# Perceiver block on one core: the experts' weight split moved into the cross-attention, five value copies moved to ScalarE, new instruction orders, a shorter rsqrt

## The chip, the cores and the metric
The kernel runs on 1 core of a Trainium2 chip. The metric is the device time of one execution in microseconds. Three runs of the kernel before took 1942.69, 1944.77 and 1945.35 us (median 1944.77).

## The reference
Three residual steps on x of 32 x 64 tokens of width 256:

```
x = x + cross_attention(layernorm(x), ctx, mask)   # ctx 32 x 1601 x 256, 16 heads of 16, masked softmax over 1601 keys
x = x + gated_causal_attention(layernorm(x))       # attn * tanh(gelu(drift * g_w1 + g_b1) @ g_w2 + g_b2); drift = gelu(layernorm(x @ dp_w1)) @ dp_w2
x = x + moe(layernorm(x))                          # 8 experts, top 2 of them, silu(a) * g @ w2[e], hidden 704
```

Weights and inputs are 32-bit floats. The experts' weights w1 (8 x 1408 x 256) and w2 (8 x 256 x 704) are wanted in two 16-bit parts, high and low, so that products of parts replace products of 32-bit floats.

## The kernel before, in words
The program has a front part (layer norm, queries), the cross-attention, the self-attention with the gate and the router's product, the routing, and the experts. Within a part every engine runs an order that is written out by hand as a string of steps; semaphores tie the engines together. TensorE, ScalarE, VectorE, GpSimd and SyncE (the queue of transfers) each take their steps strictly in order.

The cross-attention runs 32 periods, one per batch entry b, with a lead-in. Period b does the attention (S, E, L, W) of entry b, the projections and maxima (K, V, M) of entry b + 1, and the preparation of the context of entry b + 2. The steps, by engine:

- TensorE (`PE_ORDER`): K0..K7 project a piece of the keys (L696), V0..V6 two tiles of values (L708), M0..M15 a pair of score blocks for the row maxima (L723), S0..S12 a tile of transposed scores (L743, L747), W0..W12 the product of weights and values (L764 to L769), T turns the maxima (L775). K, V, M and T write into three banks of `ring`; M takes banks 0 and 1, K and V one that `K_BANK` and `V_BANK` name. A step waits until the bank's last holder has been read.
- ScalarE (`ACT_ORDER`): KH keeps the high part of a key piece (L628), E makes two exponentials of a score tile, `pT` in 32 bits (L639) and `ph` in 16 (L641), CH the high part of a context chunk (L599).
- GpSimd (`POOL_ORDER`): L makes the low part `pl = pT - ph` (L405), CL the low part of the context (L399), ADD a residual.
- VectorE (`DVE_ORDER`): KL the low part of keys (L498), VH and VL the high and the low part of values (L483, L492), X the maxima with the mask added (L535), SH and SPR the shift of the scores (L545, L551), N the normalization of the entry before, MP the mask's conversion (L560).
- SyncE: in every period the context load, the stacking of queries, 12 transfers that stack the first half of the keys, the mask, the block queries, 12 transfers for the second half, and the shift.

E(n) waits for S(n) and W(n-3); S(n) for E(n-2); W(n) for L(n). M(n) waits for X(n-1). The next period's S0 waits for the shift, and with it for SPR.

In the self-attention the steps are those of `SELF_PE`, `SELF_ACT`, `SELF_POOL`, `SELF_DVE` and `SELF_SP` over 16 tiles of 128 tokens. WL (L899 to L903), HI (L1141), LW (L1054) and WS (L932) split the experts' weights there: 24 pieces of 128 x 1408, each loaded, its high part made on ScalarE, its low part on VectorE, both stored to device memory, with two buffers. MX are the scores for the maxima, RM reads them, T and MC turn them, SH is their transfer, S, E, W and O the attention, A, WO and R its output, SU and NU the next layer norm, TU, RT and RC the router's product. The experts' part (from 1670 us) waits for all stores.

`newton_rsqrt` (L202) makes 1/sqrt on VectorE in chained steps, each waiting for the one before; it is used once ahead of the cross-attention and eight times in the self-attention (N, HN and NU).

Of the kernel before, what the change touches and what calls it, by code (L numbers as in the profile page):

```python
# [159 lines left out]
def program(nc, a, out):  # L160
    with ExitStack() as ctx:
# [59 lines left out]
        with ExitStack() as c1:  # L221
# [85 lines left out]
            with nc.Block() as block:  # L307
                @block.sync
                def _(sp):
# [47 lines left out]
                    def period(b, i, j, do_a, do_b):  # L357
                        if has_later(b):
                            load_context(b + 2)
                        if do_b:  # L360
                            stack_queries(b + 1, 1 - j)
# [1385 lines left out]
```

## Time and profile before

| | us |
|---|---|
| median of three runs | 1944.77 |
| profiled execution | 1940.98 |
| its span, first to last instruction | 1939.2 |
| turn of the maxima, first and last | 115.2 and 1377.0 |
| self-attention, first product to the end of the part | 1427 to 1638 |
| mean granted TensorE clock | 0.941 |

The span is that of one execution under the profiler; the other numbers of the document's rows are times within it, counted from its first instruction. A row of the timeline has the start, the length, the engine, the line, the operation, what it writes and reads, and how many like it are merged; in brackets stand idle time before it and what ended it. TensorE's products are pipelined, so that the distance of the starts, not the length of a row, is what one unit costs.

### The profile page before, as it was taken

What the parts mean: (1) busy time and instruction counts of PE and PEld (TensorE: products, weight loads), DVE (VectorE), ACT (ScalarE), POOL (GpSimd) and SP (SyncE); (2) the same over time, 40 slices, a digit from 0 to 9 for tenths busy, and PEclk for the clock granted to TensorE, in tenths of its full rate; (3) what the DMA queues carried; (4) which work ended last, traced back from release to release, by engine and by line L of the source; (5) the groups of instructions that cost most, each with busy time, mean ns of one, the idle gap of its engine ahead of it and who ended that gap; (6) DMA issues with size and microseconds to landing.
All of it is one profiled execution on the core that took longest, in us unless ns stands there. A gap on an engine that the chain in (4) does not pass through costs nothing. (4 is left out here: it accounts for less than half of the span.)

```text
span 1939.2 us, 59104 instructions
## 1 busy us (share of the span) xinstructions
PE 1749.3 (90%) x24652; PEld 1155.3 (60%) x24673; DVE 1384.8 (71%) x3589; ACT 1298.0 (67%) x1595; POOL 1293.0 (67%) x669
## 2 busy tenths in 40 slices
PE   3789999999999999999999999999867886599996
PEld 1346666666666666666666666666533565488885
DVE  5568888888888888788888888888467576644442
ACT  2258788887888888888878888788745543133332
POOL 1248888988888888888888888888733200244432
PEclk9779999999999999999999999999778786699998
DMA  4444445444455454544445544444156675588884
GB/s 152 167 107 116 125 135 141 126 113 129 117 154 132 109 130 114 154 130 116 123 119 153 138 112 119 123 136 107 28 170 215 200 264 191 194 250 267 248 248 126
DMA packets 169867, 290.83 MB, mean 150 GB/s; under 512 B 56450, under 2 KB 136706, under 8 KB 169442
## 3 DMA queue, kind: packets, MB, share of 16 engines
q1 hardware_dynamic: 162114, 276.83, 49.0%
q0 software_dynamic: 7488, 10.23, 2.6%
q8 instruction: 196, 3.21, 0.7%
q14 instruction: 69, 0.57, 0.1%
HBM read 169.80 MB, written 33.16 MB: 105 GB/s over the span
## 5 line engine op out<-in xcount | busy, mean ns | idle before, releaser
L405 POOL TENSOR_TENSOR pl<-pT,ph 128x1024 f16<-128x1024 f32 x416 | 882.0, 2133 | 182.4 <-ACT ph L641 182.3
L535 DVE CUSTOM_DVE_ANT_0 junk<-ring,mbias 128x804 bf16<-128x804 f32 x512 | 507.3, 991 | 170.4 <-issue 159.8
L639 ACT ACTIVATE pT<-score,lift 128x1024 f32<-128x1024 f32 (+1 forms) x416 | 464.5, 1117 | 75.0 <-PE o_acc L769 38.0
L641 ACT ACTIVATE ph<-score,lift 128x1024 f16<-128x1024 f32 (+1 forms) x416 | 464.3, 1116 | 0.0
L708 PE MATMUL ring<-wvp,cp 128*128 128x256 f16 (+1 forms) x2496 | 311.2, 276 | 4.4 <-DVE kl L498 0.5
L696 PE MATMUL ring<-cp,wkp 128*128 128x402 f16 x1536 | 307.6, 337 | 5.2 <-DVE kst L464 1.8
L708 PEld LDWEIGHTS ring<-wvp,cp 128*128 128x128 f16 (+1 forms) x2496 | 236.4, 100 | 82.3 <-issue 50.0
L399 POOL TENSOR_TENSOR cp<-cx,cp 128x804 f16<-128x804 f32 x128 | 252.4, 1992 | 49.3 <-ACT cp L599 49.3
L723 PE MATMUL ring<-kh,qm 32*128 32x402 f16 x1024 | 265.2, 338 | 19.6 <-DVE mx L535 10.2
L628 ACT ACTIVATE kh<-ring,bks 128x402 f16<-128x402 f32 x256 | 155.2, 606 | 174.7 <-PE ring L696 174.7
L769 PE MATMUL o_acc<-v,pl 128*128 128x33 f16 (+1 forms) x3328 | 242.6, 179 | 0.1
L764 PE MATMUL o_acc<-v,ph 128*128 128x66 f16 x2912 | 221.5, 192 | 6.4 <-POOL pl L405 6.4
L764 PEld LDWEIGHTS o_acc<-v,ph 128*128 128x128 f16 x2912 | 182.3, 97 | 57.5 <-issue 41.5
L769 PEld LDWEIGHTS o_acc<-v,pl 128*128 128x128 f16 (+1 forms) x3328 | 213.8, 96 | 0.7
L696 PEld LDWEIGHTS ring<-cp,wkp 128*128 128x128 f16 x1536 | 131.2, 98 | 129.6 <-DVE kl L498 21.5
L747 PEld LDWEIGHTS score<-qst,kst 64*128 64x128 f16 x6656 | 157.6, 97 | 50.1 <-issue 2.7
L483 DVE CAST v<-ring 128x512 f16<-128x512 f32 (+1 forms) x224 | 144.9, 652 | 54.2 <-PE ring L708 51.1
L743 PE MATMUL score<-delta,mbias 64*128 64x512 bf16 (+1 forms) x832 | 164.6, 392 | 11.8 <-ACT ph L641 4.7
L498 DVE SCALAR_TENSOR_TENSOR kl<-ring,bks,kh 128x402 f16<-128x402 f32 x256 | 160.2, 634 | 18.2 <-ACT kh L628 13.7
L747 PE MATMUL score<-qst,kst 64*128 64x64 f16 x6656 | 168.4, 191 | 0.0
L1369 POOL DMA_INDIRECT acc_d<-ys,to_row x39 | 64.2, 1645 | 141.4 <-DVE ys L1540 72.5
L1636 PE MATMUL score<-xp,w1p 128*128 128x256 f16 (+1 forms) x1584 | 150.9, 254 | 3.4 <-DMA w1p<-wsp 3.0
(232 smaller groups left out, 2055.1 us busy)
## 6 DMA issues: line engine op xcount, KB each, us to landing
cx<-in_ctxT SPq DMA_DIRECT2D x32, 1601.0 KB
w1p<-wsp SPq DMA_DIRECT2D x24, 1408.0 KB, 8.2
kst<-kh SPq DMA_DIRECT2D x256, 100.5 KB, 2.9
msk<-in_mask SPq DMA_DIRECT2D x64, 400.2 KB, 5.5
kst<-kh SPq DMA_DIRECT2D x256, 99.6 KB, 2.5
wsp<-w_parts SPq DMA_DIRECT2D x24, 704.0 KB, 4.3
w2p<-wsp SPq DMA_DIRECT2D x24, 640.0 KB
kst<-kl SPq DMA_DIRECT2D x128, 100.5 KB, 2.7
```

The source lines that it names most:

```text
L399: pool.tensor_tensor(cp[:, j, 1, :, chunk(n)], cx[:, :, chunk(n)], cp[:, j, 0, :, chunk(n)], ALU.subtract).then_inc(cl_ready, 1)
L405: pool.tensor_tensor(pl[:, u].rearrange("p h q -> p (h q)"), pT[:, u], ph[:, u].rearrange("p h q -> p (h q)"), ALU.subtract).then_inc(pl_r ...
L535: dve.tensor_tensor_reduce(junk[:, n % 2], ring[:, 0:2, 0:KW], mbias[:, j, 2 * KW * half:2 * KW * half + 2 * KW].rearrange("p (c k) -> p c ...
L639: act.activation(pT[0:n, u].rearrange("k (h a q) -> k a h q", a=2, q=S), scored, ACT.Exp, bias=lift[0:n, 0:1], scale=SSCALE)
L641: act.activation(ph[0:n, u].rearrange("k h (a q) -> k a h q", a=2), scored, ACT.Exp, bias=lift[0:n, 0:1], scale=SSCALE).then_inc(exp_done, 1)
L696: mm = pe.matmul(ring[:, BANK["K", k], 0:KW], wkp[:, z, cc, P * t:P * t + P], cp[:, j, y, cc, chunk(c)], start=(cc == 0 and z == y), stop= ...
L708: mm = pe.matmul(ring[0:n, BANK["V", u], D * half:D * half + D], cp[:, j, z, cc, P * kt:P * kt + n], wvp[:, y, cc, :], start=(cc == 0 and ...
L723: mm = pe.matmul(ring[:, c, 0:KW], qm[rows, j, t], kh[rows, t, chunk(2 * half + c)], start=True, stop=True)
L743: pe.matmul(score[0:n, 2 * slot + side, :], mbias[part, j, rows], delta[part, :], start=True, stop=False, skip_group_check=True)
L747: mm = pe.matmul(score[0:n, 2 * slot + side, S * p:S * p + S], kst[part, j, p, rows], qst[part, j, p, :], start=False, stop=True, skip_gro ...
L764: pe.matmul(o_acc[:, at:at + 2 * PW], high, vv.rearrange("k z w -> k (z w)"), start=(kt == 0 and p == 0), stop=last, skip_group_check=True)
L769: mm = pe.matmul(o_acc[:, at:at + PW], low, vv[:, 0, :], start=False, stop=last, skip_group_check=True)
```

## The change
The experts' weights are loaded, split and stored during the cross-attention, one of the 24 pieces in each of the periods 0 to 23, with one buffer that lies where the front part's query and value weights lay. Of the seven value copies VH of a period, ScalarE takes the numbers 0, 1, 3, 4 and 6 (6 is a single tile, the others are two), VectorE keeps 2 and 5. SyncE's order in a period becomes a string as well, with the block queries behind the shift. All other orders are new, and so are the banks. `newton_rsqrt` folds a multiplication into a fused step: 13 steps, 12 of them waited for, instead of 15. The first layer norm of the self-attention scales its 16 tiles in three runs (0 to 4, 4 to 12, 12 to 16) instead of two.

```diff
-NEWTON = 15
+NEWTON = 13
-PE_ORDER = steps("K0 S0 K1 S1 K2 V0 K3 S2 K4 M0 S3 W0 M1 S4 W1 M2 V1 M3 W2 W3 S5 M4 K5 M5 S6 S7 M6 V2 W4 M7 W5 S8 M8 K6 "
-                 "M9 W6 S9 M10 K7 M11 S10 W7 M12 W8 S11 M13 V3 M14 S12 W9 W10 M15 V4 W11 T V5 V6 W12")
-ACT_ORDER = steps("KH0 E0 KH1 KH2 E1 KH3 E2 KH4 E3 E4 CH0 E5 KH5 CH1 E6 E7 E8 KH6 CH2 E9 KH7 E10 CH3 E11 E12")
+PE_ORDER = steps("K0 V0 K1 S0 K2 M0 S1 S2 M1 K3 M2 S3 W0 M3 K4 W1 M4 S4 V1 V2 W2 K5 M5 S5 S6 M6 K6 M7 W3 W4 M8 K7 M9 S7 "
+                 "S8 M10 W5 V3 W6 V4 S9 S10 W7 M11 V5 M12 S11 W8 M13 S12 W9 M14 W10 M15 V6 W11 T W12")
+ACT_ORDER = steps("KH0 VH0 KH1 E0 KH2 E1 KH3 E2 KH4 E3 VH1 E4 KH5 CH0 E5 KH6 HI E6 KH7 E7 E8 VH3 VH4 E9 E10 E11 E12 CH1 "
+                  "VH6 CH2 CH3")
 POOL_ORDER = steps("L0 ADD L1 L2 L3 L4 L5 CL0 L6 L7 L8 L9 L10 L11 L12 CL1 CL2 CL3")
-DVE_ORDER = steps("KL0 N KL1 KL2 VH0 VL0 KL3 X0 KL4 X1 X2 VH1 X3 VL1 X4 X5 KL5 X6 VH2 X7 VL2 X8 X9 KL6 X10 X11 KL7 X12 "
-                  "X13 VH3 X14 VL3 X15 SH VH4 SPR VL4 VH5 VH6 VL5 VL6 MP")
-K_BANK, V_BANK, T_BANK = (2, 1, 2, 1, 2, 2, 2, 2), (0, 2, 2, 2, 2, 0, 1), 1
+DVE_ORDER = steps("N VL0 KL0 KL1 X0 KL2 X1 X2 KL3 X3 KL4 X4 VL1 VH2 VL2 X5 KL5 X6 X7 KL6 X8 X9 KL7 X10 LW VL3 VL4 X11 "
+                  "X12 VH5 X13 MP X14 VL5 X15 SH VL6 SPR")
+SP_ORDER = steps("WL CTX STKA MASK STKB QST SHIFT QM WS")
+K_BANK, V_BANK, T_BANK = (1, 0, 2, 2, 2, 2, 2, 2), (2, 2, 0, 2, 0, 2, 2), 0
...
-SELF_SP = steps("CA0 CB0 RO0 WL0 WL1 SK0 WS0 WL2 WL3 WS1 SQ0 SK1 WS2 WL4 WL5 WS3 SQ1 SH0 SH1 SH2 WS4 WL6 WL7 WS5 SK2 "
...
+SELF_PE = steps("X0 X1 V0 K0 K1 Q0 Q1 V1 V2 V3 X2 X3 V4 K2 K3 X4 Q2 Q3 MX0 V5 V6 V7 T0 V8 V9 MX1 X5 X6 K4 MX2 K5 T1 T2 "
+                "MX3 S0 V10 S1 V11 V12 V13 MX4 T3 Q4 Q5 MX5 T4 S2 X7 T5 MX6 W0 T6 K6 S3 W1 K7 W2 S4 W3 A0 A1 A2 WO0 WO1 "
...
+                "WO14 A15 TU5 WO15 TU6 RT5 RT6 TU7 TU8 RT7 RT8 TU9 TU10 TU11 RT9 RT10 TU12 TU13 RT11 RT12 TU14 TU15 "
+                "RT13 RT14 RT15")
+SELF_SP = steps("CA0 RO0 CB0 SK0 SQ0 SK1 SQ1 SH0 SH1 SK2 SH2 SH3 SQ2 SH4 SH5 SH6 SK3 AS0 SQ3 XS0 SH7 SH8 SH9 SH10 SH11 "
+                "SH12 AS1 SH13 SH14 XS1 SH15 AS2 XS2 AS3 XS3")
...
+            dve.tensor_scalar(ve, ve, -0.5, None, ALU.mult).then_inc(s_newton, 1)
+            chain[0] = chain[0] + 1
             step(dve.tensor_scalar(y.bitcast(I32), t.bitcast(I32), -1, 0x5F3759DF, ALU.mult, ALU.add))
             for _ in range(3):
                 step(dve.tensor_tensor(t, y, y, ALU.mult))
                 step(dve.tensor_tensor(t, t, ve, ALU.mult))
-                step(dve.tensor_scalar(t, t, -0.5, 1.5, ALU.mult, ALU.add))
-                step(dve.tensor_tensor(y, y, t, ALU.mult))
+                step(dve.scalar_tensor_tensor(y, t, 1.5, y, ALU.add, ALU.mult))
...
+            w_whole = nc.alloc_sbuf_tensor_at("w_whole", [P, WP], F32, offset=spent)
+            w_parts = nc.alloc_sbuf_tensor_at("w_parts", [P, 2, WP], F16, offset=spent + 4 * WP)
...
+                    def load_whole(q):
+                        e, k = q // PIECES, q % PIECES
+                        if q == 0:
+                            sp.wait_ge(q_done, DC * NCH)
+                            sp.wait_ge(bv_added, 1)
+                        after(sp, w_low, q)
+                        if k < DC:
+                            sp.dma_start(w_whole[:], a["w1T"][e, P * k:P * k + P]).then_inc(w_in, 16)
...
+                            elif kind == "WS" and has_piece(b):
+                                sp.wait_ge(w_low, b + 1)
+                                sp.dma_start(wsp[b // PIECES, b % PIECES], w_parts[:]).then_inc(w_out, 16)
...
+                            elif kind == "LW" and has_piece(b):
+                                dve.wait_ge(w_high, b + 1)
+                                dve.scalar_tensor_tensor(w_parts[:, 1], w_whole[:], WSCALE, w_parts[:, 0], ALU.mult, ALU.subtract).then_inc(w_low, 1)
...
+                    def keep_vh(b, j, u):
+                        n = KROWS[2 * u]
+                        tiles = min(2, KT - 2 * u)
+                        act.wait_ge(v_done, b * VU + (u + 1))
+                        after(act, pv_done, (b - 1) * KT)
+                        act.activation(v[0:n, j, 2 * u:2 * u + tiles].rearrange("k t p z w -> k (t p) z w")[:, :, 0, 0:2 * DH],
+                                       ring[0:n, BANK["V", u], 0:tiles * D].rearrange("p (h w) -> p h w", w=2 * DH), ACT.Copy).then_inc(vh_there, 1)
...
+                            elif kind == "HI" and has_piece(b):
+                                act.wait_ge(w_in, 16 * (b + 1 + (b + 1) // PIECES))
+                                after(act, w_out, 16 * b)
+                                act.activation(w_parts[:, 0], w_whole[:], ACT.Copy, scale=WSCALE).then_inc(w_high, 1)
```

## Rows read from the trace of the kernel before

**Rows 1.** Busy time by stage: cross-attention, self-attention to W0, self-attention from W0; columns named.
```profile
core 0: us, PE busy (x) PEld busy (x) DVE busy (x) ACT busy (x) POOL busy (x), PEclk, DMA share, GB/s
116.00:1378.00 1262.00, 1240.07 (x19055) 784.19 (x19054) 1028.25 (x2656) 1047.52 (x1174) 1096.81 (x538) 1.00 0.47 126
...
1427.00:1504.00 77.00, 63.75 (x525) 33.08 (x532) 55.39 (x135) 39.21 (x58) 24.00 (x15) 0.88 0.68 220
1504.00:1638.00 134.00, 111.19 (x1968) 86.37 (x1968) 81.99 (x226) 66.17 (x97) 14.02 (x11) 0.78 0.70 229
```

**Rows 2.** The line of the turn of the maxima: ns min/median/max, first and last start.
```profile
L775 PE MATMUL ring<-fold,top_m x64: 219/243/317, 115.2 to 1377.0; 128*32 128x64 f32 x64
```

**Rows 3.** Timeline of TensorE in a period (start us, length us, what).
```profile
524.65 0.20 PE L764 MATMUL o_acc<-v,ph 65*128 65x66 f16 x1
...
525.12 1.18 PE L696 MATMUL ring<-cp,wkp 128*128 128x402 f16 x6
...
526.23 0.39 PE L743 MATMUL score<-delta,mbias 64*128 64x512 bf16 x2
...
526.79 1.19 PE L696 MATMUL ring<-cp,wkp 128*128 128x402 f16 x6
...
537.45 1.49 PE L708 MATMUL ring<-wvp,cp 128*128 128x256 f16 x12
...
538.87 0.51 PE L723 MATMUL ring<-kh,qm 32*128 32x402 f16 x2
...
542.63 0.51 PE L723 MATMUL ring<-kh,qm 32*128 32x402 f16 x2
...
543.07 0.39 PE L743 MATMUL score<-delta,mbias 64*128 64x512 bf16 x2
...
543.53 0.38 PE L743 MATMUL score<-delta,mbias 64*128 64x512 bf16 x2
...
544.24 0.51 PE L723 MATMUL ring<-kh,qm 32*128 32x402 f16 x2
...
544.88 1.47 PE L708 MATMUL ring<-wvp,cp 128*128 128x256 f16 x12
...
546.18 0.19 PE L764 MATMUL o_acc<-v,ph 128*128 128x66 f16 x1
...
546.74 0.51 PE L723 MATMUL ring<-kh,qm 32*128 32x402 f16 x2
```

**Rows 4.** Timeline of ScalarE in the same period: KH0, E0, KH1, E12.
```profile
526.40 0.60 ACT L628 ACTIVATE kh<-ring,bks 128x402 f16<-128x402 f32 x1 [4.43 <-PE ring L696]
...
526.90 1.11 ACT L639 ACTIVATE pT<-score,lift 128x1024 f32<-128x1024 f32 x1
...
528.91 0.60 ACT L628 ACTIVATE kh<-ring,bks 128x402 f16<-128x402 f32 x1
...
560.34 1.11 ACT L639 ACTIVATE pT<-score,lift 65x1024 f32<-65x1024 f32 x1 [0.31 <-PE o_acc L769]
```

**Rows 5.** Timeline of VectorE in the same period: VH1, X5, KL5.
```profile
538.97 0.69 DVE L483 CAST v<-ring 128x512 f16<-128x512 f32 x1 [0.41 <-PE ring L708]
...
543.18 0.99 DVE L535 CUSTOM_DVE_ANT_0 junk<-ring,mbias 128x804 bf16<-128x804 f32 x1 [0.61 <-issue]
...
544.10 0.63 DVE L498 SCALAR_TENSOR_TENSOR kl<-ring,bks,kh 128x402 f16<-128x402 f32 x1
```

**Rows 6.** Timeline of GpSimd in the same period: L12.
```profile
562.53 2.13 POOL L405 TENSOR_TENSOR pl<-pT,ph 128x1024 f16<-128x1024 f32 x1 [0.29 <-ACT ph L641]
```

**Rows 7.** All HI and LW, by the tile they write: ns min/median/max.
```profile
L1141 ACT ACTIVATE w_parts<-w_whole x24: 1359/1368/1378, 1442.3 to 1633.9; 128x1408 f16<-128x1408 f32 x24
...
L1054 DVE SCALAR_TENSOR_TENSOR w_parts<-w_whole,w_parts x24: 1603/1626/3637, 1443.7 to 1635.3; 128x1408 f16<-128x1408 f32 x24
```

**Rows 8.** All CL by line; then one CL and the MP beside it.
```profile
L399 POOL TENSOR_TENSOR cp<-cx,cp x128: 1702/1715/2877, 18.7 to 1342.6; 128x804 f16<-128x804 f32 x128
...
525.80 2.87 POOL L399 TENSOR_TENSOR cp<-cx,cp 128x804 f16<-128x804 f32 x1
...
526.12 0.98 DVE L560 TENSOR_SCALAR mbias<-msk 128x1601 bf16<-128x1601 int32 x1
```

More of the change, by code:

```diff
@@ L119 @@
 HT = TILES // 2
-SELF_PE = steps("X0 X1 V0 Q0 K0 K1 V1 X2 X3 V2 V3 V4 V5 V6 Q1 K2 K3 V7 Q2 Q3 X4 MX0 MX1 V8 V9 T0 MX2 T1 X5 X6 V10 T2 "
[6 rows of a table removed]
-SELF_ACT = steps("XN0 XN1 XN2 XN3 XC0 XC1 QH0 XN4 KH0 XN5 XN6 XN7 KH1 XC2 XN8 XC3 XN9 HI0 XN10 XN11 HI1 QH1 KH2 KH3 HI2 "
[6 rows of a table removed]
-SELF_POOL = steps("BO0 BO1 BO2 HG0 HW0 PR0 HM0 BO3 VG0 VG1 VG2 VG3 HG1 HW1 PR1 HM1 VG4 VG5 VG6 VG7")
-SELF_DVE = steps("ST0 ST1 ST2 ST3 N0 ST4 ST5 ST6 ST7 ST8 ST9 ST10 ST11 ST12 ST13 ST14 ST15 N1 QL0 VV0 KL0 HS0 KL1 VV1 "
[8 rows of a table removed]
-SELF_SP = steps("CA0 CB0 RO0 WL0 WL1 SK0 WS0 WL2 WL3 WS1 SQ0 SK1 WS2 WL4 WL5 WS3 SQ1 SH0 SH1 SH2 WS4 WL6 WL7 WS5 SK2 "
[3 rows of a table removed]
+SELF_PE = steps("X0 X1 V0 K0 K1 Q0 Q1 V1 V2 V3 X2 X3 V4 K2 K3 X4 Q2 Q3 MX0 V5 V6 V7 T0 V8 V9 MX1 X5 X6 K4 MX2 K5 T1 T2 "
[6 rows of a table added]
+SELF_ACT = steps("XN0 XN1 XN2 XN3 XC0 XN4 XN5 XC1 XN6 XN7 KH0 KH1 QH0 QH1 XC2 XN8 XC3 XN9 XN10 XN11 KH2 KH3 XC4 XN12 "
[5 rows of a table added]
+SELF_POOL = steps("BO0 BO1 BO2 BO3 HG0 HW0 PR0 HM0 VG0 VG1 VG2 VG3 HG1 HW1 PR1 HM1 VG4 VG5 VG6 VG7")
+SELF_DVE = steps("ST0 ST1 ST2 ST3 ST4 ST5 ST6 ST7 N0 ST8 ST9 ST10 ST11 N1 ST12 ST13 ST14 ST15 N2 VV0 KL0 HS0 KL1 QL0 "
[7 rows of a table added]
+SELF_SP = steps("CA0 RO0 CB0 SK0 SQ0 SK1 SQ1 SH0 SH1 SK2 SH2 SH3 SQ2 SH4 SH5 SH6 SK3 AS0 SQ3 XS0 SH7 SH8 SH9 SH10 SH11 "
+                "SH12 AS1 SH13 SH14 XS1 SH15 AS2 XS2 AS3 XS3")
 SELF_USES = [use for use in SELF_PE if use[0] in ("X", "Q", "K", "V", "T", "A", "TU")]
@@ L182, in program @@
         ln_ve, ln_y, ln_t = (sb(f"ln_{w}", [P, TILES]) for w in ("ve", "y", "t"))
+        spent = -(-nc.sbuf_base // 32) * 32
+        xn = sb("xn", [P, 2, D])
         xn_d = nc.dram_tensor("xn_d", (TOK, D), F32).ap()
@@ L252, in program @@
             hold_v = sb1("hold_v", [P, 2])
-            junk = sb1("junk", [P, 2, 2, KW], BF16)
+            junk = sb1("junk", [P, 2, KW], BF16)
             mx = sb1("mx", [P, PAIRS, 3])
@@ L285, in program @@
             x2_ready = sem("x2_ready")
+            w_in, w_high, w_low = sem("w_whole_in"), sem("w_high_parts"), sem("w_low_parts")
             CONSTS = [(ident[:], a["ident"]), (sel_q[:], a["sel_q"]),
@@ L302, in has_later, with has_piece @@
                 return not (isinstance(b, int) and b + 2 >= B)
+            def has_piece(b):
+                return 0 <= b < E * PIECES
             def chunk(n):
@@ L357, in period @@
                     def period(b, i, j, do_a, do_b):
[L358 to L361, printed above, removed]
-                            stack_keys(b + 1, 1 - j, 0)
-                        if has_later(b):
-                            load_mask(b + 2)
-                            load_block_queries(b + 2, j)
-                        if do_b:
-                            stack_keys(b + 1, 1 - j, 1)
-                            shift_queries(b + 1, 1 - j)
+                        for kind, n in SP_ORDER:
+                            if kind == "CTX" and has_later(b):
+                                load_context(b + 2)
+                            elif kind == "QST" and do_b:
+                                stack_queries(b + 1, 1 - j)
+                            elif kind == "STKA" and do_b:
+                                stack_keys(b + 1, 1 - j, 0)
+                            elif kind == "MASK" and has_later(b):
+                                load_mask(b + 2)
+                            elif kind == "QM" and has_later(b):
+                                load_block_queries(b + 2, j)
+                            elif kind == "STKB" and do_b:
+                                stack_keys(b + 1, 1 - j, 1)
+                            elif kind == "SHIFT" and do_b:
+                                shift_queries(b + 1, 1 - j)
+                            elif kind == "WL" and has_piece(b):
+                                load_whole(b)
+                            elif kind == "WS" and has_piece(b):
+                                sp.wait_ge(w_low, b + 1)
+                                sp.dma_start(wsp[b // PIECES, b % PIECES], w_parts[:]).then_inc(w_out, 16)
                     shift_rows = a["shift_row"][0:PAIRS * NK].partition_broadcast(STRIP)
@@ L488, in keep_vl @@
                         tiles = min(2, KT - 2 * u)
-                        dve.wait_ge(vh_kept, b * VU + (u + 1))
+                        if u in VH_ACT:
+                            dve.wait_ge(vh_there, b * len(VH_ACT) + VH_ACT.index(u) + 1)
+                        else:
+                            dve.wait_ge(vh_kept, b * len(VH_DVE) + VH_DVE.index(u) + 1)
                         parts = v[0:n, j, 2 * u:2 * u + tiles].rearrange("k t p z w -> k (t p) z w")
@@ L647, in period @@
                                 keep_kh(b + 1, i + j, 1 - j, n)
+                            elif kind == "VH" and do_b:
+                                keep_vh(b + 1, 1 - j, n)
                             elif kind == "E" and do_a:
                                 exponentiate(b, j, n)
+                            elif kind == "HI" and has_piece(b):
+                                act.wait_ge(w_in, 16 * (b + 1 + (b + 1) // PIECES))
+                                after(act, w_out, 16 * b)
+                                act.activation(w_parts[:, 0], w_whole[:], ACT.Copy, scale=WSCALE).then_inc(w_high, 1)
                             elif kind == "CH" and has_later(b):
@@ L856, in program @@
                 first2_in, consts2_in, rows2_in = sem("first2_in"), sem("consts2_in"), sem("rows2_in")
-                w_in, w_out = [sem(f"w_whole_in{j}") for j in range(2)], [sem(f"w_parts_out{j}") for j in range(2)]
-                w_high, w_low = sem("w_high_parts"), sem("w_low_parts")
                 stats_made, moments_made = sem("stats_made"), sem("moments_made")
@@ L1136, in _ @@
                                 act.activation(xt2[:, n % 2], bank("TU", n)[:, 0:D].rearrange("p (c k) -> p c k", c=DC), ACT.Copy).then_inc(yt_ready, 1)
-                            elif kind == "HI":
-                                e, k, j = n // PIECES, n % PIECES, n % 2
-                                act.wait_ge(w_in[j], 16 * sum(1 if q % PIECES < DC else 2 for q in range(j, n + 1, 2)))
-                                after(act, w_out[j], 16 * (n // 2))
-                                act.activation(w_parts[:, j, 0], w_whole[:, j], ACT.Copy, scale=WSCALE).then_inc(w_high, 1)
                     @block.tensor
@@ L1337, in load @@
                                          whole[:, z, (FT - 1) * D:WP].rearrange("(r h) f -> r h f", h=2)).then_inc(w2_in[j], 16)
-                    for j in range(2):
-                        sp.wait_ge(w_out[j], 16 * (E * PIECES // 2))
+                    sp.wait_ge(w_out, 16 * E * PIECES)
                     sp.wait_ge(te_ready, 1)
```

41 lines of the change are left out of this document (13 added, 28 removed), and 38 rows, old and new, of tables (SELF_ACT, SELF_DVE, SELF_PE, SELF_SP).

## The prediction
> **What bounds the kernel now.** I read the page's busy shares first (TensorE 90% of the span, VectorE 71, ScalarE and GpSimd 67), then the busy time by stage, then the cross-attention instruction by instruction, and at last the self-attention. The stage rows say where the busy time lies: in the 1262 us of the cross-attention it is busy 98% at full clock, while GpSimd has 87%, ScalarE 83% and VectorE 81%; in the 211 us of the self-attention (1427 to 1638) it has 83%, at a granted clock of 0.88 and 0.78 [rows 1]. The cross-attention repeats one written order per batch entry; the turn of the maxima (step T) comes at 115.2 first and at 1377.0 last, 31 intervals, so a period takes 40.70 us, and 31 full periods make two thirds of the time [rows 2]. So 1 us per period is worth 31 us, as much as anything the self-attention can give.
>
> Inside a period I need two kinds of numbers. How long TensorE's units are, from start to start (the thirteen rows are W12, K0, S0, K1, V1, M3, M5, S6, S7, M6, V2, W4 and M7) [rows 3]: K 1.11 before S, S 0.56 (0.46 before another S), V 1.42 before M and 1.30 before W, M 0.44, W 0.56 (0.47 before K). And the handovers: KH starts 1.28 after its K, E 0.67 after its S, an E (two exponentials) takes 2.01 [rows 4]; a value copy starts 1.52 after its V, a maximum X starts 0.55 after its M, the next M not before 1.06 after X, and a KL behind an X starts 0.92 after it [rows 3, 5]. L starts 2.19 after its E [rows 4, 6] and takes 2.09. Two recurrences follow: M after M never under 1.61, and K after K in one bank never under 1.28 + 0.63 (KH's length and a handover) + 0.69 (KL's) = 2.6.
>
> **The change, part by part: cross-attention.** With these lengths the old order sums to 39.0 us of TensorE without a wait (8 K 8.9, 7 V 8.8, 16 M 7.1, 13 S 7.1, 13 W 6.9, T 0.2), the new one to 38.4: S stands before S four times instead of once, and three W stand before V. That is one bound: 2.3 us less per period.
>
> ScalarE now does 33.6 us per period (1047.5 us over 31.2 periods [rows 1]). Added are value copies VH0, 1, 3, 4 and the single-tile VH6. Their length lies between 0.60 for 402 columns and 1.11 for 1024 [rows 4], so 0.69 for 512; overlapped like their neighbours, 0.58 each and 0.37 for VH6: 2.7 us. HI, in 24 periods, is 1.37 [rows 7], 1.3 overlapped. So ScalarE holds some 37.5 us of work, in one order, and every item waits for a TensorE unit that itself waits for earlier ones.
>
> I therefore walk the new order from K0 = 0 with the handovers above. TensorE: K0 0, V0 1.0, K1 2.3, S0 3.5, K2 4.0, M0 5.2, M1 6.8 (its predecessor's X), K3 7.5 (KL2, which is behind E0 and KH2), K4 10.8, V1 13.4, K5 16.5, M6 19.2, K6 19.8, M8 22.6, K7 23.1, M10 25.9, V3 26.8, V4 28.55. Eleven waits of 0.02 to 0.26 us by then, together 1.4. ScalarE: E0 4.1 (it was 1.8 after K0 [rows 3, 4]), E3 12.6, VH1 14.9, E4 15.5, KH5 17.7, CH0, E5 19.0, KH6 21.1, HI 21.6, E6 22.9, E7 25.4, E8 27.4, VH3 29.4, VH4 30.1 (V4 + 1.52), then E9 30.65, E10 32.65, E11 35.1 (it needs W8's end, W8 starts at 34.4), E12 37.1. GpSimd: L11 37.3, L12 39.4, done 41.5. TensorE's W12, the period's last unit, starts at 41.6 and K0 of the next period at **42.07**. In the old order E12 started 35.2 after K0 and L12 37.4 [rows 3, 4, 6]. So the packed TensorE order does not decide: the chain V4, VH4, E9 to E12, L12, W12 does. HI itself is not what costs; without it E6 and E7 wait for W3 and S7, and E8 begins at 27.4 all the same. I count all 31 periods alike.
>
> Beside it VectorE: seven VH become two (-3 us), LW adds 1.63 in 24 periods [rows 7], so its 33 us fall to about 32. But two of its instructions meet GpSimd. The mask step MP took 0.98 us and the CL that it met 2.87, where the median CL takes 1.72 [rows 8]. In the old order MP ran while only CLs ran, off the path. The new order has MP between X13 and X14, at 36.5 to 37.4, in the middle of L10: plus up to 1.16 us on the chain L10, L11, L12, W12. LW took 3.64 us instead of 1.6 when it met a GpSimd instruction [rows 7]; at 27.3 it lies beside L7, and either waits or makes L7 late by 1.3, which W7 to W9 feel in part. With both in full the walk ends at 43.1; with neither at 42.07. I take **42.6**, the middle, since part of such a delay falls into waits already counted. MP before X14 also makes M15 0.8 late.
>
> The Trainium skill has a rule here: "SBUF — State Buffer", section "SBUF: two separate sides", calls the pair of ports that VectorE and GpSimd share an exclusive lock, held for a whole instruction, the loser blocking fully. The trace agrees for LW (3.64 against 1.6). For MP the record shows the other order, GpSimd's instruction longer and MP not. By the rule MP could instead wait for all of L10, up to 2.1 us, and the period would be some 43 us, 12 us more in all than I take.
>
> Queues: SP issues in a new order. SHIFT is 3.9 us ahead of the S0 that needs it, against 2.6 before, so a late landing should stall it less often than before; I count nothing for that. QM comes behind SHIFT, 4 us before M0. WL and WS add 1.4 MB per period, some 36 GB/s on 126 at a DMA share of 0.47 [rows 1]; the context load, issued at about 5.8, has 12 us until CH0. Nothing for it, up to +0.5 per period if the queue backs up. WL waits only for the LW of the period before, long done.
>
> Cross-attention: 31 x (42.6 - 40.7) = **+59 us**. Bounds: TensorE's packing alone would give 31 x -2.3 = -71, excluded by ScalarE, whose chain alone, with TensorE never late, ends W12 at 40.3 and the period at 40.8 (+3); above, 43.4 (+84).
>
> **Self-attention.** 24 LW (24 x 1.63 = 39 us of VectorE, more where they meet GpSimd) and 24 HI (24 x 1.37 = 33 us of ScalarE) leave [rows 7], with 48 transfers' issues on SP. The full-clock work of TensorE is 63.75 x 0.88 + 111.19 x 0.78 = 143 us of 211 [rows 1]; 36 us are idle, 32 are half clock. New order up to W0: the first key and query stacks no longer stand behind WS and WL on SP, MX0 comes 6 us sooner, and the gate's chain (hd, gelu, drift, tanh) lets W0 start 64 us after the stage's first X instead of 77 (the two windows are cut at W0): -13. After it: 134 us were 87 of work and 47 of idle and clock. Five more units of work stand there now, idle time falls by a third as LW no longer sits before the maxima RM, and the last TU and RT still run at half clock, eleven pairs instead of sixteen: 120 us, -14. Together **-27 us**. Bounds: -12, if the waits pass to the stacks and the gate, and -40, all of LW.
>
> **rsqrt** in 12 chained steps of 15, one call more (three N for two): -1 us, most of it hidden. Later loads by the experts wait for te_ready, not for the pieces: 0.
>
> Sum: 1941.0 (the profiled execution; 1939.2 of it are the span) + 59 - 27 - 1 = 1972. The runs' median lies 3.8 above it; I predict **1975** for the median.
>
> **Rivals.** (1) Not slower: handovers shorter than I walk, MP and LW between GpSimd's instructions, so that the period is ScalarE's own 40.8, and the self-attention's gain stands: 1941 + 3 - 27 - 1 = 1916, median 1920. It decides from where the period stays under 41.6, which is 40.7 + (27 + 1) / 31. For it: the new order is just in time at many places (K5, M5, S8, M11 within 0.1 us of their releasers), so small errors of mine add up; against it: the constants reproduce the old period's M6, M5 and K6 to 0.1 us. (2) The walk without contention and with half its small waits, 41.5: +25 - 27 - 1 = -3, median 1942, about even. (3) The pieces move but the self-attention stays bound by its chains (stacks, gate, half clock): gain 12 only, with 42.6: 1987, median 1991; for it, its DMA waits are few beside the idle time that TensorE's own half clock makes.
>
> **How the numbers follow.** Forecast (42.1 to 43.1) 0.58, with its own range 1955 to 1992; rival 3 0.07; rival 1 0.23; rival 2 0.12, split evenly among faster, same and slower. What a measurement can tell from no change is about 0.2%, 4 us. Faster 0.23 + 0.04 = 0.27, same 0.06 (with the edges), slower 0.67. Range 1916 to 1996.
>
> **What would show it.** Right: the interval from T to T at 42 to 43 us; TensorE waiting for pl before W12 and W10 in each period; E9 starting 30 us or more after K0; an L of over 3 us beside each MP; LW over 2 us in many periods; TensorE busy below 95% there. In the self-attention no LW before RM, W0 about 64 us after the first X, end about 184 us after it. Wrong: T to T under 41.2, or the self-attention shorter by over 35 us.

## The result, and the profile after

The changed kernel takes **2018.72 us** (median of 4 runs, 2017.03 to 2021.36) against 1944.55 us: 1.0384 times as long (95% interval 1.0366 to 1.0402), 74 us slower. The prediction had the sign and less than half of the size: 1975, range 1916 to 1996. The profiled execution took 2020.34 us (span 2018.5), 79.4 more than that of before.

Busy time by stage, as in [rows 1]: the cross-attention, the self-attention from the first transposition of x to W0, and from there to its last router product.

```profile
core 0: us, PE busy (x) PEld busy (x) DVE busy (x) ACT busy (x) POOL busy (x), PEclk, DMA share, GB/s
115.00:1491.00 1376.00, 1313.06 (x19048) 820.54 (x19047) 995.85 (x2523) 1163.82 (x1355) 1111.73 (x540) 0.92 0.51 141
...
1540.80:1606.00 65.20, 58.84 (x483) 30.38 (x490) 36.54 (x111) 29.59 (x50) 20.68 (x14) 0.93 0.33 85
1606.00:1715.30 109.30, 102.98 (x2016) 77.77 (x2016) 58.95 (x205) 47.05 (x82) 14.09 (x13) 0.92 0.22 64
```

The turn of the maxima, the row that answers to [rows 2]:

```profile
L832 PE MATMUL ring<-fold,top_m x64: 219/314/317, 114.5 to 1491.0; 128*32 128x64 f32 x64
```

So a period takes (1491.0 - 114.5) / 31 = 44.40 us instead of 40.70: +115 us. The self-attention takes 174.5 us instead of 207.8 (-33); the rest is 2 us shorter. 115 - 33 - 2 = 80.

The stage row also shows what the prediction does not have: the granted clock, 1.00 in the cross-attention before, is 0.92, and T itself takes 0.31 us in the median instead of 0.24. TensorE is still busy 95% of the stage (1313 of 1376 us), since work at half clock counts as busy. Finer windows: the first period after T, then 6.8 us and the 37.5 us behind them from a later one.

```profile
116.00:157.00 41.00, 38.54 (x594) 24.18 (x592) 28.99 (x67) 36.53 (x43) 32.80 (x16) 0.99 0.52 145
```
```profile
778.80:785.60 6.80, 6.45 (x53) 4.12 (x54) 5.45 (x21) 3.52 (x6) 6.80 (x5) 0.50 0.10 35
785.60:823.10 37.50, 35.85 (x564) 22.33 (x562) 26.93 (x63) 34.14 (x40) 29.07 (x14) 1.00 0.62 171
```

In every period but the first the clock falls to its lower level (0.50, which is 1.2 GHz) for 6.8 us, around the period's end and the next one's K0 and V0. The first period, without a fall of its own, took 42.7 us, what I had forecast; the others 43.6 to 46.0. What TensorE did before it fell stands in the timeline (start us, length us, what, in brackets the idle time before):

```profile
773.09 4.22 POOL L441 TENSOR_TENSOR pl<-pT,ph 128x1024 f16<-128x1024 f32 x2
...
776.61 1.56 DVE L599 TENSOR_SCALAR mbias<-msk 128x1601 bf16<-128x1601 int32 x1
...
777.47 4.76 POOL L441 TENSOR_TENSOR pl<-pT,ph 128x1024 f16<-128x1024 f32 x2 [0.15 <-ACT ph L683]
...
779.15 0.85 PE L780 MATMUL ring<-kh,qm 32*128 32x402 f16 x2 [1.14 <-DVE mx L574]
...
779.92 1.49 PE L765 MATMUL ring<-wvp,cp 128*65 128x256 f16 x6
```

MP (L599) starts at 776.61, 0.7 us before GpSimd's L10 ends (L9 and L10 are the first line), and takes 1.56 us instead of 0.98; M15 waits 1.14 us for the X14 behind it; the clock falls in that gap, and M15 already takes 0.85 us for 0.51, as the single-tile V6 1.49 for 0.8. GpSimd's L11 and L12 beside MP take 4.76 us together, where two take 4.2. On the page of the profile the waits of M (L780) for VectorE are 48.9 us, over a microsecond per period:

```profile
L780 PE MATMUL ring<-kh,qm 32*128 32x402 f16 x1024 | 272.3, 346 | 58.3 <-DVE mx L574 48.9
```

### The profile page after: what moved, and what is told of

It reads as the page before. It is cut to its first block and busy times, and to the rows that moved or that the text cites. A ratio compares the mean times of both kernels' runs of the same rounds, so it can differ in the third digit from the quotient of the medians.

```text
span 2018.5 us, 59318 instructions
## 1 busy us (share of the span) xinstructions
PE 1806.3 (89%) x24652; PEld 1179.8 (58%) x24673; DVE 1310.1 (65%) x3425; ACT 1387.0 (69%) x1757; POOL 1300.0 (64%) x669
## 5 line engine op out<-in xcount | busy, mean ns | idle before, releaser
L441 POOL TENSOR_TENSOR pl<-pT,ph 128x1024 f16<-128x1024 f32 x416 | 926.4, 2240 | 269.4 <-ACT ph L683 265.7
L753 PE MATMUL ring<-cp,wkp 128*128 128x402 f16 x1536 | 338.3, 361 | 10.2 <-DVE kst L500 1.8
L765 PE MATMUL ring<-wvp,cp 128*128 128x256 f16 (+1 forms) x2496 | 341.3, 292 | 3.1 <-DVE v L531 0.7
L780 PE MATMUL ring<-kh,qm 32*128 32x402 f16 x1024 | 272.3, 346 | 58.3 <-DVE mx L574 48.9
L765 PEld LDWEIGHTS ring<-wvp,cp 128*128 128x128 f16 (+1 forms) x2496 | 254.2, 107 | 84.0 <-issue 44.3
L435 POOL TENSOR_TENSOR cp<-cx,cp 128x804 f16<-128x804 f32 x128 | 216.9, 1713 | 64.3 <-ACT cp L641 64.3
L826 PE MATMUL o_acc<-v,pl 128*128 128x33 f16 (+1 forms) x3328 | 256.5, 184 | 0.0
L531 DVE TENSOR_TENSOR v<-ring,v 128x512 f16<-128x512 f32 (+1 forms) x224 | 146.1, 653 | 160.2 <-ACT v L692 159.1
L821 PEld LDWEIGHTS o_acc<-v,ph 128*128 128x128 f16 x2912 | 195.9, 102 | 60.2 <-POOL pl L441 28.3
L826 PEld LDWEIGHTS o_acc<-v,pl 128*128 128x128 f16 (+1 forms) x3328 | 227.0, 98 | 4.9
L692 ACT ACTIVATE v<-ring 128x512 f16<-128x512 f32 (+1 forms) x160 | 89.0, 558 | 101.9 <-PE ring L765 99.2
```

What stands on the lines that cost most here:

```text
L435: pool.tensor_tensor(cp[:, j, 1, :, chunk(n)], cx[:, :, chunk(n)], cp[:, j, 0, :, chunk(n)], ALU.subtract).then_inc(cl_ready, 1)
L441: pool.tensor_tensor(pl[:, u].rearrange("p h q -> p (h q)"), pT[:, u], ph[:, u].rearrange("p h q -> p (h q)"), ALU.subtract).then_inc(pl_r ...
L753: mm = pe.matmul(ring[:, BANK["K", k], 0:KW], wkp[:, z, cc, P * t:P * t + P], cp[:, j, y, cc, chunk(c)], start=(cc == 0 and z == y), stop= ...
L765: mm = pe.matmul(ring[0:n, BANK["V", u], D * half:D * half + D], cp[:, j, z, cc, P * kt:P * kt + n], wvp[:, y, cc, :], start=(cc == 0 and ...
L780: mm = pe.matmul(ring[:, c, 0:KW], qm[rows, j, t], kh[rows, t, chunk(2 * half + c)], start=True, stop=True)
L821: pe.matmul(o_acc[:, at:at + 2 * PW], high, vv.rearrange("k z w -> k (z w)"), start=(kt == 0 and p == 0), stop=last, skip_group_check=True)
```

## The experiments

Theory A: a gap on TensorE late in the period makes the clock fall, and the half clock costs 1.7 us per period on top of the order's own cost and of MP beside L11. Rival R: only contention and the engines' chains count. Rival R2: the pieces themselves (HI, LW, their loads and stores) make the period long. Time of before in these runs: 1943.6 to 1947.4 us.

**1. MP moved back** to the end of VectorE's order:
```
-... X12 VH5 X13 MP X14 VL5 X15 SH VL6 SPR")
+... X12 VH5 X13 X14 VL5 X15 SH VL6 SPR MP")
```


> One edit to the changed kernel: the mask step MP goes from before X14 to the end of VectorE's order, where it stood before. Theory A (the clock): M15 waits 1.15 us for X14, which stands behind MP, in every period; the granted clock falls to 0.5 there for 6.8 us and this costs 1.7 us per period, MP beside L11 another 0.6. Then the clock stays at 1.0 in the cross-attention, M15 waits under 0.5 us, L11 takes 2.13 us instead of 2.68, and T comes every 42.0 to 42.3 us instead of 44.4: 2020 - 31 x 2.2 = 1952 us (1945 to 1960). Rival R (only contention and ScalarE's chain count, the clock falls for other reasons and costs nothing on this path): only the 0.6 us go, T every 43.8 us, about 2001 us.

Measured: 2012.82 us, ratio 1.0349 (1.0328 to 1.0369). Neither. T comes every 44.16 us, and the clock still falls, now among these waits of TensorE:

```profile
774.00 0.51 PE L780 MATMUL ring<-kh,qm 32*128 32x402 f16 x2 [0.36 <-DVE mx L574]
774.69 1.04 PE L765 MATMUL ring<-wvp,cp 128*65 128x256 f16 x6 [0.18 <-DVE v L531]
...
777.36 0.24 PE L821 MATMUL o_acc<-v,ph 65*128 65x66 f16 x1 [0.61 <-POOL pl L441]
```
```profile
775.10:781.90 6.80, 6.19 (x55) 4.20 (x54) 5.14 (x19) 3.17 (x5) 6.80 (x5) 0.50 0.40 120
1266.00:1308.00 42.00, 39.48 (x609) 24.89 (x606) 30.34 (x82) 36.77 (x43) 35.40 (x19) 1.00 0.47 124
```

The gap at M15 went from 1.14 to 0.36 us, yet the clock fell: at 775.10, behind the waits of 0.36 and 0.18 us; the one of 0.61 us before W12 lies in the fall. In the one period without a fall (from 1266) K0 came back after 42.4 us, in its neighbours after 44.2 and 43.8.

**2. The gap filled, MP left where it is:**
```
-... W9 M14 W10 M15 V6 W11 T W12")
+... W9 M14 W10 D M15 V6 W11 T W12")
+ "D": for _ in range(10): pe.matmul(score[:, 2 * (1 - j), 0:D], wkp[:, 0, 0, 0:P], wvp[:, 0, 0, :], ...)
```


> The changed kernel with work that nothing needs: ten matmuls of 256 columns (1.07 us at full clock) on TensorE between W10 and M15, in the gap in which TensorE waits for X14; they write a scores buffer that is free, and MP stays where it is. Theory A: it is the gap that makes the clock fall. The clock stays at 1.0 in the cross-attention, the contention of MP stays, T comes every 42.6 to 42.8 us, 2020 - 31 x 1.7 = 1967 us (1962 to 1973). Rival R: T every 44.4 us or a little later, 2020 us or more. If the gap ahead of V6 and W12 is enough by itself, the clock still falls and the time is 2018 to 2025 us.

Measured: 1987.25 us, ratio 1.0216 (1.0197 to 1.0236): 31 us faster by work that nobody needs. In 20 of 31 intervals the clock stayed up and T came after 42.5 to 42.8 us, as expected; in 11 it fell for 3.4 us, and T came after 44.2 to 44.7. The same order, the same MP: against the 44.4 us of the changed kernel this is the price of the clock by itself, 44.4 - 42.8 = 1.6 us per period. The remaining wait before W12 (0.83 us) ends just before each of these falls and could be what starts them; experiment 3 fills it.

```profile
115.00:370.00 255.00, 244.13 (x3710) 154.32 (x3710) 191.31 (x475) 225.80 (x264) 212.72 (x102) 1.00 0.55 154
```

**3. Both places filled, MP last:**
```
-... W9 M14 W10 M15 V6 W11 T W12")
+... W9 M14 W10 D4 M15 V6 W11 T D8 W12")
```

> The changed kernel with MP at the end of VectorE's order, and matmuls that nothing needs in both idle places of TensorE that are left: four before M15 (0.43 us), eight before W12 (0.86 us). What the runs so far say: with MP last there still was a wait of 0.36 us before M15 and one of 0.6 us before W12, and the granted clock still fell for 6.8 us in each period (T every 44.4 us; in the one period without a fall 42.4); with only the gap before M15 filled and MP in its place, periods without a fall took 42.8 us. Theory A: the clock stays at 1.0, MP's contention is gone too, T every 42.1 to 42.4 us, 2020 - 31 x 2.15 = 1953 us (1948 to 1960). Rival: the clock falls in a third of the periods or more whatever is filled (it is not the idle time), 1975 us or more.

Measured: 1955.96 us, ratio 1.0047 (1.0029 to 1.0064), T every 42.26 us, not one fall in the cross-attention:

```profile
114.00:1423.00 1309.00, 1273.22 (x19410) 805.85 (x19408) 981.72 (x2523) 1161.01 (x1355) 1119.20 (x540) 1.00 0.54 148
```

Theory A holds, R is out: against experiment 1 nothing is different but twelve useless matmuls in waits, and 57 us are gone. That a gap of a certain length starts a fall does not follow, as experiment 5 shows.

**4. The same with the pieces' work all but gone:**
```
 HI, LW: -w_whole[:]  +w_whole[:, 0:WP if b == 0 else 8]   (w_parts alike)
```

> As fill_both, but after the first piece HI and LW convert 8 of the 1408 columns (the other columns of the pieces are left as they were; loads and stores stay): what the pieces' work costs in the new order when the clock stays at 1.0. My walk says HI costs nothing and LW beside L7 (3.39 us instead of 2.13) is taken up before L11: T every 42.0 to 42.2 us against 42.2, 0 to 5 us less in all, 1951 to 1956 us. Rival R2 (the pieces are what makes the period long): T at 41.2 or less, 1925 us or less.

From the second piece on this kernel converts 8 of the 1408 columns and leaves out the rest; only its time counts. Measured: 1956.91 us, ratio 1.0070 (1.0044 to 1.0097); T every (1425.8 - 116.7) / 31 = 42.23 us. HI and LW cost the new order nothing when the clock stays up. Loads and stores stayed in; what they cost in this order no run shows. In the old order (experiment 12) most periods with a piece take 40.5 us, loads and stores included, as most of those of before do without.

**5. The gap put into the kernel before** (the same place for MP there):
```
-... X13 VH3 X14 VL3 X15 ... VL5 VL6 MP")
+... X13 VH3 MP X14 VL3 X15 ... VL5 VL6")
```


> The kernel before with one edit: MP goes from the end of VectorE's order to before X14, so that M15 is late by about 1 us. Theory A: the gap on TensorE makes the clock fall for 6.8 us in every period here too; the delay costs 0.8 to 1.2 us and the half clock another 1 to 2, T every 42.3 to 43.6 us instead of 40.7, 1990 to 2030 us. Rival R (a delay is only a delay): the clock stays at 1.0, T every 41.5 to 41.9 us, 1966 to 1978 us.

Measured: 2008.11 us, ratio 1.0334 (1.0301 to 1.0367). One step of 1 us, moved by a few places, costs 61 us. M15 waits 1.10 us in each period (3.38 in one); the clock falls in 12 of 31, mostly every second, for 3.4 us (6.8 in the one with the long wait):

```profile
1009.25 0.53 PE L723 MATMUL ring<-kh,qm 32*128 32x402 f16 x2 [1.10 <-DVE mx L535]
```
```profile
1009.60:1013.00 3.40, 3.23 (x25) 2.29 (x25) 1.84 (x7) 0.32 (x1) 3.40 (x3) 0.50 0.61 159
1013.00:1094.90 81.90, 78.63 (x1210) 49.00 (x1207) 64.98 (x167) 67.48 (x76) 66.87 (x34) 1.00 0.46 122
```

Most intervals without a fall are 41.9 (the delay: +1.2), with one of 3.4 us 43.3 to 43.7 (+1.4 more). So "in every period" was wrong, the mechanism was not.

**6. Is it the chain W8, E11, E12, L12, W12?** As experiment 3, with
```
-... M11 V5 M12 S11 W8 M13 ...
+... M11 V5 S11 W8 M12 M13 ...
```

> As fill_both, and S11 and W8 go ahead of M12 on TensorE. In my walk of the period E11 waits for the end of W8, which stands behind V5, M12 and S11; in the runs without a fall of the clock E11 starts 0.5 us after E10 is done. Theory A (the chain W8, E11, E12, L12, W12 ends the period): E11 0.4 to 0.55 us earlier, T every 41.6 to 41.9 us, 0.5 less than fill_both, 15 us in all: 1938 us (1932 to 1948). Rival: the maxima X12 to X15, now 1.0 us later behind M12, hold M15 and V6 back by as much, and the period stays at 42.2 or grows: 1953 to 1965 us.

Measured: 2024.24 us, ratio 1.0400 (1.0380 to 1.0419). A miss of 86 us. E11 did start 0.44 us earlier; but M12 and M13 now touch, M13 waits for X12, and that new gap brings the clock down 20 times (T every 44.40, 43.1 at best):

```profile
774.41 0.51 PE L780 MATMUL ring<-kh,qm 32*128 32x402 f16 x2 [1.10 <-DVE mx L574]
```

I had counted the M behind it late, but not the hole that this makes. That E12, L12 and W12 end the period shows here from the other side: where the clock stays up, T comes after 43.1 us, 0.9 later than in experiment 3, and L12 starts 1.15 later in the median. That E11 ahead of them decides is not shown.

**7. The old cross-attention orders with the pieces in them:**
```
 PE:  ... V0 S2 K3 K4 S3 M0 W0 S4 M1 W1 ...  (was V0 K3 S2 K4 M0 S3 W0 M1 S4 W1)
 ACT: ... CH3 E11 E12 HI VH5 VH6
 DVE: KL0 MP N KL1 ... SH VH4 SPR VL4 LW VL5 VL6
 SP:  WL CTX QST STKA MASK QM STKB SHIFT WS
```

> The changed kernel with the cross-attention's orders and banks of the kernel before, and the pieces fitted into their idle places: HI and the value copies VH5 and VH6 on ScalarE after E12, LW on VectorE after VL4, MP behind KL0, S2, S3 and S4 one place earlier on TensorE; the self-attention's orders are the new ones. Theory A and my walk: TensorE stays dense, the clock stays at 1.0, T every 41.0 to 41.5 us (40.7 and some 0.5 for half a microsecond more of VectorE work at the period's start), so 1941 + 31 x 0.6 - 33 - 2 = 1925 us (1912 to 1940), faster than both kernels. Rival R2 (the pieces themselves, their loads, HI and LW, are what makes the period longer, wherever they stand): T at 43 us or more, 1978 us or more.

Measured: 1978.02 us, ratio 1.0160 (1.0135 to 1.0186), T every 42.92 us (42.5 without a fall). This is 53 us above the forecast, and the time that R2 gave (1978 or more); but experiments 8 and 12, with the same pieces, are faster than before, so it is not the pieces themselves. MP was the largest mistake. Behind KL0 it meets GpSimd's CL2 and waits for its end: 2.18 us in the median for 0.98, and K3 waits 1.0 us for KL1, half of the 2.0 us by which an undisturbed period is longer than the 40.5 of before. The rest are new waits of 0.5 us before M2 and 0.4 before K1; no run separates them.

```profile
417.74 4.13 POOL L434 TENSOR_TENSOR cp<-cx,cp 128x804 f16<-128x804 f32 x2
...
418.12 2.18 DVE L598 TENSOR_SCALAR mbias<-msk 128x1601 bf16<-128x1601 int32 x1
```

**8. Old cross-attention untouched, LW in four parts in the next period:**
```
 ACT: ... CH3 E11 E12 HI"
 DVE: ... X1 LW0 X2 VH1 X3 VL1 X4 LW1 X5 KL5 X6 LW2 VH2 ... X10 LW3 X11 ..."
 SP:  "CTX QST STKA MASK QM WS WL STKB SHIFT"
```


> The cross-attention's orders, banks and MP exactly as in the kernel before, no value copy on ScalarE; the pieces in its idle places: HI on ScalarE after E12 (3.2 us idle there), LW in four parts of 352 columns in the next period, in VectorE's gaps of 0.5 to 0.6 us before X2, X5, VH2 and X11; the store and the next load on the queue before STKB. Self-attention and rsqrt as in the changed kernel. Theory A: HI is hidden, each LW part (about 0.45 us by 1.62/4) fits its gap or is 0.1 late, TensorE stays dense and the clock at 1.0: T every 40.7 to 41.2 us, 1941 + 31 x 0.2 - 33 - 2 = 1912 us (1904 to 1925), faster than both kernels. Rival R2 (a part of LW of over 0.6 us beside GpSimd's L, or the load landing too late for HI, opens gaps on TensorE and the clock falls again): T at 42 us or more, 1950 us or more.

Measured: 1928.80 us, ratio 0.9910 (0.9891 to 0.9928): faster than both kernels, 17 us above the forecast. T every 41.45 us, two falls. Three parts take mostly 0.52 to 0.60 us; the one behind X6 starts 0.3 us after CL0 and takes 1.79, and M8 is late:

```profile
L620 DVE SCALAR_TENSOR_TENSOR w_parts<-w_whole,w_parts x96: 519/556/1801, 169.8 to 1144.5; 128x352 f16<-128x352 f32 x96
```

**9. The same with the old self-attention orders** (`SELF_PE`, `SELF_ACT`, `SELF_POOL`, `SELF_DVE`, `SELF_SP` of before, less WL, HI, LW and WS):

> As old_cross_quarters, but with the self-attention's orders of the kernel before, out of which only the pieces' steps (WL, HI, LW, WS) are taken; so the difference to old_cross_quarters is what the new search of the self-attention's orders brings, and the rest of the 33 us is what the pieces' leaving brings. By the lengths (24 LW of 1.63 on VectorE, which stood before the maxima) I expect the leaving to be most of it: self-attention 180 to 185 us from first transposition to last router product instead of 174.5, so 6 to 10 us slower than old_cross_quarters, 1918 to 1922 us with the cross-attention as expected there. Rival: the orders are what matters, the time is 20 us or more above old_cross_quarters.

Measured: 1949.08 us, ratio 1.0007 (0.9997 to 1.0017): the rival. The stage takes 193.7 us instead of 170.2; the windows of the two kernels, old orders first:

```profile
1450.00:1643.70 193.70, 169.35 (x2475) 115.59 (x2496) 93.51 (x311) 74.56 (x130) 34.74 (x26) 0.85 0.24 70
```
```profile
1451.30:1621.50 170.20, 158.17 (x2475) 106.77 (x2496) 95.31 (x315) 76.47 (x132) 34.78 (x26) 0.94 0.27 74
```

Taking the pieces away, with the shorter rsqrt that this run keeps, is worth 207.8 - 193.7 = 14 us, the new orders with the layer norm in three runs 23, and with them the granted clock rises from 0.85 to 0.94.

**10 to 12. LW's parts placed better.** First the part behind X6 to behind X12, store and load behind STKB:
```
 DVE: -X6 LW2 VH2 ... X10 LW3 X11 KL7 X12   +X6 VH2 ... X10 LW2 X11 KL7 X12 LW3
 SP:  -QM WS WL STKB SHIFT                  +QM STKB WS WL SHIFT
```

> As old_cross_quarters, with one of LW's four parts moved: it stood behind X6, where it met GpSimd's CL0 and took 1.79 us where the others took 0.52 to 0.60; now it stands behind X12, where GpSimd is idle for 0.8 us, and the store and the next load go behind STKB on the queue. Theory A: all four parts take 0.5 to 0.6 us, the 0.7 us that M8 was late go, T every 40.5 to 40.7 us with pieces (40.4 without) instead of 41.1, and fewer falls of the clock: 1929 - 24 x 0.6 = 1914 us, with the 5 to 8 us that the clock took there 1908 (1905 to 1918). Rival: the parts still open gaps ahead of X5 and X11 of a tenth each that add up, and the load now lands too late for HI, which then delays KH0: T at 41.1 or more, 1926 to 1935 us.

Measured: 2073.89 us, ratio 1.0641 (1.0616 to 1.0667). The rival, in a worse form: behind the 12 issues of STKB the load lands after the period's end, and KH0 stands behind HI, which waits for it. All 24 HI waited, 8.7 us each. TensorE's long wait is that of S0, 4.8 us in the median: S0 needs the shift, which now stands behind the load on the queue and takes 5.1 us in the median from issue to landing, instead of 1.9 in experiment 8:

```profile
L706 ACT ACTIVATE w_parts<-w_whole x24: 1376/1377/1377, 163.4 to 1257.6; 128x1408 f16<-128x1408 f32 x24
...
  ACT w_parts L706: 208.9, 24
```
```profile
592.23 0.61 PE L800 MATMUL score<-delta,mbias 64*128 64x512 bf16 x2 [4.78 <-issue]
```

Then with the queue as in 8, and a small first part behind VL0:
```
 DVE: VH0 VL0 LW0 KL3 X0 KL4 X1 LW1 X2 ... X4 LW2 X5 ... X6 VH2 ... X10 LW3 X11
```

> As old_cross_quarters, with LW in four unequal parts, all ahead of the store and the next load, which stay in front of STKB on the queue (behind STKB the load landed 6 us too late): 176 columns behind VL0, where VectorE waits 0.37 us and GpSimd is idle, 400 behind X1, 432 behind X4, 400 behind X10; the part behind X6, which met CL0 and took 1.79 us, is gone. By 352 columns in 0.52 us and 1408 in 1.62, a part takes 0.15 us and 1.04 ns per column: 0.34, 0.57, 0.60, 0.57. Theory A: each fits its gap or is 0.1 us late, M8 is no longer 0.7 us late, T every 40.5 to 40.8 us with pieces instead of 41.1, few or no falls of the clock: 1929 - 24 x 0.4 = 1919 us, 5 to 8 us less if the clock stays at 1.0: 1914 (1906 to 1922). Rival: the first part meets L1 or the others open small gaps that add up, T at 41.1 or more, 1926 us or more.

Measured: 1936.90 us (1928.39 to 1943.07), ratio 0.9949 (0.9931 to 0.9967). The rival again: 40.7 us where all fits, but in some periods the part of 176 columns starts just behind L1 and waits for all of it, M0 comes 1.6 us late, and the clock falls in 6 periods for 6.8 us:

```profile
L620 DVE SCALAR_TENSOR_TENSOR w_parts<-w_whole,w_parts x96: 331/643/2093, 165.7 to 1154.0; 128x400 f16<-128x400 f32 x48, 128x176 f16<-128x176 f32 x24, 128x432 f16<-128x432 f32 x24
```

At last three parts:
```
 DVE: ... X1 LW0 X2 ... X4 LW1 X5 ... X6 VH2 ... X10 LW2 X11 ...
+part = slice((0, 472, 944)[n], (472, 944, WP)[n])
```

> As old_cross_quarters, with LW in three parts (472, 472 and 464 columns, 0.64 us each by 0.15 us and 1.04 ns per column) in the three places where no run has shown one wait for GpSimd: behind X1, X4 and X10. The part behind X6 (1.79 us beside CL0) and the one behind VL0 (up to 2.09 us beside L1) are gone. Theory A: each part is 0.1 us longer than its gap, T every 40.7 to 40.9 us with pieces, no fall of the clock or one or two: 114 + 31 x 40.75, the rest as in old_cross_quarters (527.8), 1905 + 2: 1907 us for the profiled execution, 1905 to 1916 for the median. Rival: a part of 0.64 us is late enough to wait for L2, L4 or L8 in some periods, gaps of over 1 us follow and the clock falls there: 1922 us or more.

Measured: **1908.21 us** (1907.79 to 1912.33), ratio **0.9822** (0.9805 to 0.9838), faster than both kernels and as forecast. No part waits for a whole L (0.94 us at most), T comes every 40.93 us (40.5 in most intervals), the clock falls once:

```profile
L620 DVE SCALAR_TENSOR_TENSOR w_parts<-w_whole,w_parts x72: 644/723/944, 168.7 to 1128.9; 128x472 f16<-128x472 f32 x48, 128x464 f16<-128x464 f32 x24
```
```profile
114.00:1383.00 1269.00, 1240.36 (x19051) 784.21 (x19050) 1073.30 (x2727) 1077.53 (x1198) 1095.87 (x538) 1.00 0.54 152
```

## Why the prediction was right in sign and wrong in size

**The walk of the order was right.** Starts in us after K0, as predicted and as medians over 14 periods of the traces:

| | walk | fill_both | changed kernel |
|---|---|---|---|
| K1 | 2.3 | 2.33 | 3.59 |
| M1 | 6.8 | 6.84 | 8.10 |
| V1 | 13.4 | 13.51 | 14.77 |
| K5 | 16.5 | 16.59 | 17.85 |
| V4 | 28.55 | 28.69 | 29.96 |
| E9 | 30.65 | 30.76 | 32.03 |
| E12 | 37.1 | 37.32 | 38.59 |
| L12 | 39.4 | 39.59 | 41.42 |
| W12 | 41.6 | 41.79 | 43.68 |

With the clock up and MP away it is 0.2 us off at the end (42.26 against 42.07). The packed TensorE order indeed does not decide. That L11, L12 and W12 end the period, experiments 2 and 3 show: L11 is 0.55 us longer in the one, and so is the period. For E9 to E11 there is only the agreement with the walk.

**The step that failed** is the one under all of them: every length was taken at full clock, because before the cross-attention had it throughout [rows 1]. "MP before X14 also makes M15 0.8 late" stood there as an aside without a price. The wait was 1.14 us, since MP also waited for L10, and the clock fell in it. It was not this wait alone: with MP moved away the smaller ones were enough (experiment 1). What failed is that no wait on TensorE, counted or not, had a price in clock. The changed kernel is 1.26 us behind fill_both at K1, since K0 and V0 run at half clock, keeps that to E12, loses 0.56 more at L12 and 0.3 around W12. So the term of 31 x (42.6 - 40.7) = +59 us, measured:

- the new order by itself, 42.26 - 40.70 = 1.56 us: +48
- MP beside L11 and before X14, 42.81 - 42.26 = 0.55: +17
- the clock, 44.40 - 42.81 = 1.59: **+49, not in the sum**

The first two are 65 against my 59. The split goes by kernels whose useless matmuls differ (ten in one place, twelve in two).

**Contention.** Expected 1.16 for MP and 1.3 for LW, half of it felt. MP cost 0.55 and lengthened L11 to 2.68, not to over 3. It did both things that I had set against each other: it began in L10, took 1.56 us instead of 0.98, ended 0.86 after L10, and held up L11. LW starts 0.2 us before L7 (medians 28.74 and 28.96 after K0), takes 1.62, and L7 3.39 us; "LW over 2 us in many periods" was wrong (maximum 1.622), and its 1.26 us on L7 are taken up before L11 (experiment 4). The Trainium skill, "SBUF — State Buffer", section "SBUF: two separate sides", says that where a GpSimd instruction meets a VectorE instruction with two inputs in SBUF, or in a mode that takes both port pairs, whichever starts first has the shared ports for its whole length. The runs agree from both sides: LW first, L7 longer by 1.26; CL0, CL2, L10 or L1 first, and LW's part takes 1.79 for 0.52, MP 2.18 or 1.56 for 0.98, a part 2.09 for 0.33. The MP of before, which was not delayed inside a CL [rows 8], still does not fit, and no run explains it.

**HI costs nothing:** right (42.23 against 42.26). **SP's new order, nothing:** right; neither HI nor LW waited in the changed kernel. What a queue can cost was shown by old_cross_clear: 145 us above experiment 8, 25 falls of the clock among them.

**Self-attention:** -33 against -27, inside the bounds. W0 came 65.2 us after the first x (expected 64), the stage's rest took 109 (expected 120). Why was half wrong: I gave most of it to LW and HI leaving; that is 14 us, and the new orders are some 20. The granted clock is higher with them (0.92 against 0.82 in the stage); how much of the 20 us is clock no run separates.

**The rivals.** ScalarE's own 40.8 was out of reach, and 41.5 too; none of my four cases had the clock in it, and the upper bound of 43.4 us was no bound, since it held every length fixed. The range was also narrower than its own terms: +84 and -12 make 1941 + 84 - 12 - 1 = 2012, with the 3.8 of the median 2016, not 1996; that this is near the measured 2019 is chance, for the clock is in neither. One reading was off as well: 1262 us are 31.0 periods, not 31.2, so ScalarE did 33.8 us per period, not 33.6; no other term hangs on it.

What stays open is the condition. A gap of 1.1 us brought the clock down in 30 of 31 periods of the changed kernel and in 12 of 31 of before_with_gap; fill_idle had the same order in all periods and fell in 11. Neither the length of one gap nor its place decides alone.

## What to carry to other kernels

In a kernel that keeps TensorE busy nearly all the time, a wait of a microsecond has two prices: its length, and the half clock that may follow; look at the granted clock of single periods, not at the stage's mean, and price each new wait on TensorE at both. Before believing that a chain of other engines sets a period, fill TensorE's waits with matmuls that nothing needs: if that makes the kernel faster, as it did here by 31 and 57 us, the clock is in it. Work added to VectorE goes in pieces that fit its gaps, in places where no GpSimd instruction has just begun; a piece that starts just behind one can wait for all of it (0.52 us became 1.79, 0.33 became 2.09).
